# Indices as 16-bit words, and another order of the prologue, in a linear-attention and table-weight layer on eight cores

## What is computed

```python
xn = layernorm(x)
Q = relu(xn @ Wq.T + bq) * decay[n];  K = relu(xn @ Wk.T + bk) * decay[n];  V = xn @ Wv.T + bv
KV = K.T @ V (per head);  Ksum = K.sum(tokens)
att = ((Q @ KV) / (Q @ Ksum + 1e-6)) @ Wo.T + bo
h = silu(xn @ lut[gate_idx].T) * (xn @ lut[up_idx].T)
y = x + att + h @ lut[down_idx].T
```

## Time and profile before

| what | us |
|---|---|
| median of 3 runs (2285.55 to 2312.48) | 2286.12 |
| the profiled execution | 2286.72 |
| its span, slowest core (5) | 2285.1 |
| spans of the eight cores | 2258.1 to 2285.1 |
| TensorE busy | 2113.8 |
| VectorE busy | 1933.5 |
| ScalarE busy | 2006.8 |

### The profile page before, as it was taken

How to read it: one execution, slowest core, us unless ns; L and a number is a source line. 1 busy time by engine, 2 the same in 40 slices (tenths; PEclk the granted TensorE clock), 3 DMA queues, 4 the chain that set the end, 5 groups by cost and what they waited for, 6 DMA issues and landing times.

```text
span 2285.1 us, 32191 instructions; the slowest of 8 cores (2258.1 to 2285.1 us)
## 1 busy us (share of the span) xinstructions
PE 2113.8 (93%) x10561; PEld 985.8 (43%) x10561; DVE 1933.5 (85%) x2274; ACT 2006.8 (88%) x1203; POOL 208.2 (9%) x346
## 2 busy tenths in 40 slices
PE   3999999999989999997899999999999999998965
PEld 1444444444444444443344444444444444443422
DVE  4687888899889898996798999999997898888885
ACT  4799988899889988997699999999999989898895
POOL 2000000000000000001000000000000020202030
PEclk8999999999999999998999999999999999999987
DMA  9961122221222212224724333333336565554522
GB/s 214 199 137 47 57 73 79 79 79 62 77 83 79 88 61 78 79 79 85 137 79 130 119 126 124 122 128 117 130 121 170 149 165 175 145 174 129 152 88 97
DMA packets 71750, 257.74 MB, mean 113 GB/s; under 512 B 9314, under 2 KB 9442, under 8 KB 66338
## 3 DMA queue, kind: packets, MB, share of 16 engines
q0 software_dynamic: 35296, 128.73, 21.2%
q1 hardware_dynamic: 36290, 126.96, 17.3%
HBM read 213.71 MB, written 76.02 MB: 127 GB/s over the span
## 4 chain that ended last, share of the span: by engine, by line
PE 41%; DVEq 23%; DVE 13%; ACT 9%; DMA 6%; issue 6%; SPq 0%; ACTq 0%; POOL 0%; POOLq 0%
PE kvb L964 16%; DVEq L380 13%; PE pp L486 9%; ACT pln L340 8%; PE pp L499 7%; DVE wdec L381 7%; DVEq L508 4%; DVEq L353 3%; PE pp L964 3%; DMA gi<-gidx 3%; DVE st L393 2%; PE pp L945 2%; DVE code L359 2%; DVEq L394 1%; DMA xt<-xb 1%
## 5 line engine op out<-in xcount | busy, mean ns | idle before, releaser
L340 ACT ACTIVATE pln<-gi,bi,sc 128x2048 uint16<-128x2048 int8 x903 | 1832.1, 2086 | 192.2 <-DVE wdec L381 189.8
L381 DVE TENSOR_TENSOR wdec<-wdec,pln 128x2048 uint16<-128x2048 uint16 x903 | 1137.3, 1260 | 128.7 <-ACT pln L340 54.2
L964 PE MATMUL kvb<-xown,wring 128*128 128x512 bf16 x2304 | 508.4, 379 | 0.5 <-DMA wring<-wh 0.5
L486 PE MATMUL pp<-wk_bf,xmid 128*128 128x512 bf16 x1536 | 354.6, 385 | 39.3 <-DVE kbuf L511 38.7
L499 PE MATMUL pp<-wv_bf,xmid 128*128 128x512 bf16 x1536 | 347.2, 379 | 0.7 <-ACT vbuf L518 0.7
L964 PEld LDWEIGHTS kvb<-xown,wring 128*128 128x128 bf16 x2304 | 223.2, 98 | 260.1 <-issue 1.0
L989 PE MATMUL kvb<-w3r,hT 128*128 128x512 bf16 x860 | 216.9, 387 | 51.1 <-DMA w3r<-wh 51.1
L486 PEld LDWEIGHTS pp<-wk_bf,xmid 128*128 128x128 bf16 x1536 | 146.2, 99 | 208.1 <-issue 53.7
L499 PEld LDWEIGHTS pp<-wv_bf,xmid 128*128 128x128 bf16 x1536 | 148.1, 98 | 171.8 <-issue 2.8
L311 POOL DMA_DIRECT2D gi<-gidx x119 | 66.6, 560 | 1522.1 <-ACT pln L340 986.7
L363 DVE TENSOR_SCALAR wdec<-code,hi,lo 128x2048 uint16<-128x2048 uint8 x102 | 138.0, 1353 | 21.5 <-DMA wh<-wdec 6.1
(11 more groups left out here) (112 smaller groups left out, 1446.5 us busy)
## 6 DMA issues: line engine op xcount, KB each, us to landing
wh<-wdec POOLq DMA_DIRECT2D x121, 512.0 KB, 2.9
wring<-wh SPq DMA_DIRECT2D x86, 512.0 KB, 3.4
xt<-xb SPq DMA_DIRECT2D x32, 1024.0 KB, 6.5
gi<-gidx POOLq DMA_DIRECT2D x119, 256.0 KB, 3.0
w3r<-wh SPq DMA_DIRECT2D x43, 512.0 KB, 4.9
wk_bf<-wk POOLq DMA_DIRECT2D x16, 512.0 KB, 31.6
wv_bf<-wv POOLq DMA_DIRECT2D x16, 512.0 KB, 48.6
wq_bf<-wq POOLq DMA_DIRECT2D x16, 512.0 KB, 18.1
```

Source lines behind the costliest of these rows:

```text
L340: scalar.activation(out[:], gi[k % 2][:], AF.Abs, bias=bi8[:, p : p + 1], scale=sc8[:, p : p + 1]).then_inc(s_pl, 1)
L381: vector.tensor_tensor(wdec[k % 2][:], wdec[k % 2][:], pln[(7 * k + m) % NS][:], ALU.min).then_inc(s_mn, 1)
L486: i = tensor.matmul(kb[:], xT(t, dc), wk_bf[:, j, dc, :], start=(dc == 0), stop=(dc == DC - 1))
L964: i = tensor.matmul(bank[g % 6][:], wring[k % 3][:, dc * 128 : (dc + 1) * 128], xown[:, dc, h2 * 512 : (h2 + 1) * 512], start=(dc == 0), s ...
```

## The change

The host doubles each index byte, so that an index is a 16-bit word and a tile's load 512 KB, not 256. The code pass is one AND and OR over 1024 32-bit words: each word becomes a bf16 number whose exponent holds the pair and whose last bit is the bit. The scale of plane i is multiplied by 2^(38-4i), and the bias is the same for all. The pair pass XORs into wdec itself and works there on 16-bit words; the buffer code7 is gone. PL_PRO becomes 8.

In the prologue SyncE loads x0, eye, indices 0, x1 to x3, indices 1, and then dk, bq, epc; tiles 4 to 7 wait only for a free slot. POOL's wv quarter 0 waits for x2, the next quarters for x5. The second half of the transposed tiles 0 to 3 is copied by ScalarE. The transposes of the next tile stand in the middle of a K or V product. VectorE waits for dk before tile 0. Cut to its core (not shown: `v_mm` as `k_mm`; ebase, bi8, sc8 and swi; own_evict_b's choice of engine; the same regrouping on ScalarE and VectorE for tiles 5 to 7, where planes 7 and 8 are made one each):

```diff
-PL_PRO = 10
+PL_PRO = 8
...
-        gi = [sb(es, f"gi{i}", [128, D], I8) for i in range(2)]
+        gi = [sb(es, f"gi{i}", [128, 2 * D], I8) for i in range(2)]
...
-                scalar.activation(out[:], gi[k % 2][:], AF.Abs, bias=bi8[:, p : p + 1],
+                scalar.activation(out[:], gi[k % 2][:].bitcast(BF16), AF.Abs, bias=bi8[:, p : p + 1],
...
-            vector.scalar_tensor_tensor(w32, w32, 4, w32, ALU.logical_shift_left, ALU.bitwise_or)
-            vector.drain()
-            vector.tensor_scalar(w32, w32, -0x1E1E1E1F, None, ALU.bitwise_and).then_inc(s_e, 1)
+            vector.tensor_scalar(w32, w32, 0x0E010E01, 0x30003000, ALU.bitwise_and,
+                                 ALU.bitwise_or).then_inc(s_e, 1)
...
         def dec_pair(vector, k):
-            w32 = gi[k % 2][:].bitcast(I32)
-            vector.drain()
-            vector.tensor_tensor(code7[:], w32, swi[:, 0:1].to_broadcast([128, 512]), ALU.bitwise_xor)
-            vector.drain()
+            w = wdec[k % 2]
             if k >= 2:
                 wh_done(vector, k - 2)
-            vector.tensor_scalar(wdec[k % 2][:], code7[:].bitcast(U8), hi7[:, 0:1], lo7[:, 0:1],
-                                 ALU.mult, ALU.max)
+            vector.drain()
+            vector.tensor_tensor(w[:].bitcast(I32), gi[k % 2][:].bitcast(I32),
+                                 swi[:, 0:1].to_broadcast([128, 1024]), ALU.bitwise_xor)
+            vector.drain()
+            vector.tensor_scalar(w[:], w[:], hi7[:, 0:1], lo7[:, 0:1], ALU.mult, ALU.max)
...
-        def k_mm(tensor, u):
+        def k_mm(tensor, u, nxt=None):
...
+                if nxt is not None and dc == 8:
+                    own_pe(tensor, nxt)
...
             def _(sync):
...
-                for k in range(2):
-                    dec_idx(sync, k)
                 sync.dma_start(out=eye_sb[:], in_=eye_in).then_inc(s_eye, 16)
+                dec_idx(sync, 0)
+                for t in range(1, 4):
+                    sync.dma_start(out=xts[t][:], in_=xb[t * 128 : (t + 1) * 128, :]).then_inc(s_x[t], 16)
+                dec_idx(sync, 1)
                 sync.dma_start(out=dk_sb[:], in_=dkc).then_inc(s_dk, 16)
...
-                for t in range(1, NT):
-                    if t in (2, 3):
-                        sync.wait_ge(s_wk0[2 * t - 4], 16)
-                    elif OT > t >= 4:
+                for t in range(4, NT):
+                    if t < OT:
                         sync.wait_ge(s_xn, 2 * (t - 3))
...
                 gpsimd.dma_start(out=bk_bf[:, 0:512], in_=bk[:, 0:512]).then_inc(s_bk0, 16)
+                gpsimd.wait_ge(s_x[2], 16)
...
                     if j == 1:
-                        gpsimd.wait_ge(s_k, 1)
+                        gpsimd.wait_ge(s_x[1], 32)
...
             def _(scalar):
...
+                for t in range(4):
                     ln_root(scalar, t)
-                    dec_act(scalar, (3, 5, 6, 8)[t - 1])
                     ln_norm_act(scalar, t)
+                    if t > 0:
+                        scalar.wait_ge(s_sc8, 1)
+                        dec_act(scalar, t + 1)
                     own_evict_a(scalar, t)
+                    own_evict_b(scalar, t)
+                ln_root(scalar, 4)
+                ln_norm_act(scalar, 4)
+                dec_act(scalar, 6)
+                v_evict(scalar, 0)
+                own_evict_a(scalar, 4)
...
             def _(vector):
...
                 dec_code(vector, 0)
-                ln_stats(vector, 0)
-                ln_scale(vector, 0)
-                own_evict_b(vector, 0)
                 vector.wait_ge(s_dk, 16)
-                for t in range(1, 5):
+                for t in range(4):
                     ln_stats(vector, t)
                     ln_scale(vector, t)
-                    dec_dve(vector, (3, 5, 6, 8)[t - 1])
+                    if t > 0:
+                        dec_dve(vector, t + 1)
                     if t == 2:
                         vector.wait_ge(s_bk0, 16)
-                    if t in (2, 3):
+                    if t >= 2:
                         k_evict(vector, t - 2)
-                    own_evict_b(vector, t)
...
             def _(tensor):
...
-                for t in range(4):
-                    own_pe(tensor, t)
-                    if t == 0:
-                        tensor.wait_ge(s_sc8, 1)
-                    k_mm(tensor, t)
-                v_mm(tensor, 0)
-                own_pe(tensor, 4)
+                own_pe(tensor, 0)
+                tensor.wait_ge(s_sc8, 1)
+                for t in range(3):
+                    k_mm(tensor, t, t + 1)
+                k_mm(tensor, 3)
+                v_mm(tensor, 0, 4)
...
-        "gidx": gidx, "lut16": f32(L0_ffn_lut).reshape(1, 16),
+        "gidx": np.repeat(gidx, 2, axis=2), "lut16": f32(L0_ffn_lut).reshape(1, 16),
```

More of the change, by code:

```diff
@@ L102, in build @@
     bo = nc.dram_tensor("bo", [128, D], F32, kind="ExternalInput").ap()
[L103 removed]
+    gidx = nc.dram_tensor("gidx", [NK, 128, 2 * D], I8, kind="ExternalInput").ap()
     lut16 = nc.dram_tensor("lut16", [1, 16], F32, kind="ExternalInput").ap()
@@ L421, in own_evict_a, with own_evict_b @@
             scalar.copy(xT_half(t, 0), ps_t[:]).then_inc(s_xa, 1)
-        def own_evict_b(vector, t):
-            vector.wait_ge(s_t, 2 * t + 2)
-            vector.tensor_copy(xT_half(t, 1), ps_u).then_inc(s_xb, 1)
+        def own_evict_b(eng, t):
+            eng.wait_ge(s_t, 2 * t + 2)
+            if t < 4:
+                i = eng.copy(xT_half(t, 1), ps_u)
+            else:
+                i = eng.tensor_copy(xT_half(t, 1), ps_u)
+            i.then_inc(s_xb, 1)
         def own_pe(tensor, t):
@@ L488, in k_mm, with v_mm @@
             i.then_inc(s_k, 1)
-        def v_mm(tensor, u):
+        def v_mm(tensor, u, nxt=None):
             t, j = unit(u)
@@ L674, in _ @@
                 for i in range(8):
-                    gpsimd.memset(ebase[:, i : i + 1], float(32 * i if i < 4 else 32 * i - 256))
+                    gpsimd.memset(ebase[:, i : i + 1], float(2.0 ** (38 - 4 * i)))
                 for i in range(2):
@@ L754, in _ @@
                 v_evict(scalar, 2)
+                dec_act(scalar, 8)
+                ln_root(scalar, 6)
                 own_evict_a(scalar, 5)
-                dec_act(scalar, 10)
-                ln_root(scalar, 6)
                 v_evict(scalar, 3)
@@ L760, in _ @@
                 for u in range(4, NU):
+                    if u in (4, 5):
+                        own_evict_a(scalar, u + 2)
+                    if u == 4:
+                        ln_root(scalar, 7)
+                        ln_norm_act(scalar, 7)
                     if u > 28 and u % 4 == 1 and u < NU - 4:
@@ L799, in _ @@
                 vector.wait_ge(s_cst, 1)
-                vector.tensor_tensor(bi8[:], sc8[:], ebase[:], ALU.mult)
+                vector.scalar_tensor_tensor(bi8[:], sc8[:], -128.0, pr[:, :, 0], ALU.mult, ALU.subtract)
                 vector.drain()
-                vector.scalar_tensor_tensor(bi8[:], bi8[:], -1.0, pr[:, :, 0], ALU.mult, ALU.subtract)
+                vector.tensor_tensor(sc8[:], sc8[:], ebase[:], ALU.mult)
                 vector.tensor_tensor(hi7[:], pr[:, 7:8, 0], pr[:, 7:8, 1], ALU.max)
@@ L840, in _ @@
                         vector.wait_ge(s_bk, 16)
-                    k_evict(vector, u)
                     p, r = OT + (u - 28) // 4, (u - 28) % 4
                     if u == 4:
-                        dec_dve(vector, PL_A[4] - 1)
                         ln_stats(vector, 7)
-                        own_evict_b(vector, 6)
+                    if u in (4, 5):
+                        own_evict_b(vector, u + 2)
+                    if u == 4:
                         ln_scale(vector, 7)
-                    elif u == 5:
-                        dec_dve(vector, PL_A[5] - 1)
-                        own_evict_b(vector, 7)
+                    k_evict(vector, u)
+                    if u in (4, 5):
+                        pass
                     elif u >= 28 and p < NT and r >= 2:
@@ L920, in _ @@
                 kv_mm(tensor, 1)
-                own_pe(tensor, 5)
-                v_mm(tensor, 3)
+                v_mm(tensor, 3, 5)
                 kv_mm(tensor, 2)
                 for u in range(4, NU):
-                    k_mm(tensor, u)
+                    k_mm(tensor, u, u + 2 if u < 6 else None)
                     p, r = OT + (u - 28) // 4, (u - 28) % 4
@@ L930, in _ @@
                     kv_mm(tensor, u - 1)
-                    if u in (4, 5):
-                        own_pe(tensor, u + 2)
                 tensor.wait_ge(s_ke, NU)
```

38 lines of the change are left out of this document (13 added, 25 removed).

## The result

The changed kernel takes 2305.86 us (median of 20 runs) where the kernel before, run beside it, takes 2286.22: a ratio of 1.0061, 95% interval [1.0033, 1.0089]. That is inside the 2% that count as no change, but the interval leaves out 1, so the change costs some 14 us; 2286.1 x 1.0061 is 2300.

What follows compares the result with a forecast made beforehand. VectorE was taken to set the projections by a little, TensorE gate and up, ScalarE's decode the down stage. Terms +20 - 14 + 6 + 2 = +14 us on 2286.7 gave 2301, by the median 2300; range 2270 to 2322.

Steps and rivals of the forecast that it cites:

- Prologue, +20: Prologue: statistics of tile 0 wait for dk, landing at 42 us behind larger loads; +20 us (+4 to +24).
- Codes, -14: Projections: cheaper code passes and an unchanged pair cost relieve VectorE; -14 us over 24 token tiles (4 to 21 saved).
- rival 2: VectorE's pair pass stays at two elements per cycle, so projections win 5 us, not 14: 2311 us; chance 0.18.
- two thirds that were to reach the path: Projections: of 0.86 us less VectorE work per token tile, two thirds, 0.58 us, were to shorten the time.
- Q stage, +6: Start of the Q stage: wq is issued behind a later tile 53, and tile 54 comes later; +6 us (0 to +10).
- Gate and up, 0: Gate and up: TensorE is fully busy, so a faster VectorE buys nothing; 0 us.
- Down, +2: Down stage: two more planes +4, VectorE's relief -3, doubled index load +1; +2 us in all (-4 to +9).
- VectorE's relief there shortens ScalarE's small waits: -3: Down stage: less VectorE work was to shorten ScalarE's small waits, 43.0 us before; -3 us.
- +1 for the doubled load: Down stage: the index load of twice the size beside output traffic was to cost +1 us.
- Rival 1: Prologue: dk lands early and tile 1 lands 10 us sooner, so -10 in place of +20: 2270 us; chance 0.10.
- Rival 3: Every tile: doubled index loads over 5 us hold up the code pass; 46 us on top at 6.6 us, 2346; chance 0.08.
- Rival 4: ScalarE reads bf16 at another price; 0.1 us per plane, 20 us either way in the down stage: 2280 or 2320; chance 0.06.

Runs made afterwards that it cites:

- late wait: The changed kernel with VectorE's wait for dk moved to the first K eviction, where dk is first read: 2275.93 us, ratio 0.9964.
- order-only kernel: The changed kernel with one-byte indices and the old code and pair passes, so only prologue order and PL_PRO 8: 2313.44 us, ratio 1.0129.
- codes alone: The kernel before with 16-bit indices and the new code and pair passes, old prologue and PL_PRO 10: 2272.76 us, ratio 0.9949.
- doubled pass: The changed kernel with every code pass made twice, the second leaving the words as they are: 2339.21 us, ratio 1.0245.
- kernel with the codes and tile 1 first: Old kernel with new codes, eye before the indices, tile 1 before the second index load, dk waited for at first use: 2263.98 us, ratio 0.9911.
- early load: The changed kernel with SyncE issuing dk right behind eye, ahead of the first index load; VectorE's wait unmoved: 2280.38 us, ratio 0.998.
- in pairs: Kernel with the codes and tile 1 first, GpSimd's eight bias additions per quarter spread two behind each of four index tiles: 2258.25 us, ratio 0.9871.

## Why the prediction was right

The forecast was 2300 us, range 2270 to 2322. The median, 2305.86, lies in it, and the ratio gives 2300. The mechanisms of the prologue and of the codes held by themselves; that the sum comes out to the microsecond is partly luck, since several terms were off and cancelled, and one step was wrong.

*Prologue, +20.* Measured +19.0, behind the mechanism named: statistics at 37.91, not 42, ended by the landing of dk. dk took 32.0 us from issue to landing where the sum gave 36. What was too long is the 8.2 us for two small transfers: in the trace the second index load, the last big one ahead of dk, lands at 35.4 (33.9 in the sum) and dk 2.3 us behind it. From dk on, K of tile 0 came 8.75 us later (8.6 forecast) and K of tile 3 38.7 (38). K of tile 4, forecast 26.7 us behind, came 31.3 behind. That term was short by 4.6 and hid that dk's was long by 4: 107.91 against 107, and 139.26 against 137 for tile 8. The late wait shows the same without any stall on dk, 29.3 us against 25.4, so it is the new order itself that is slower there; by what, no run shows. The order-only kernel has the same +18.9, the late wait takes 22.1 back (299.5 to 277.4).

*Codes, -14.* Measured -11.1, and -12.7 with the codes alone. The code pass takes 686 ns (forecast 705), the XOR 1226 (1240), and the TENSOR_SCALAR over the u16 tile:

```profile
L362 DVE TENSOR_SCALAR wdec<-wdec,hi,lo x102: 810/812/1604, 87.9 to 2264.5; 128x2048 uint16<-128x2048 uint16 x102
```

812 ns, where 810 was taken from the argument that the streaming part halves. So the pair costs 2.04 us, as before (the medians were 692 and 1346 ns), and rival 2 (two per cycle) falls. The Trainium skill's rule of four per cycle (VectorE: DVE Perf Modes, What auto-detection actually checks) agrees with the fall from 1346 to 812 ns. The Trainium skill's 693 ns for 2048 elements (VectorE: DVE Perf Modes, Side-by-side: where the cycles go for N=2048 bf16) is 0.12 us less than this form takes, with two operands read from pointers. The two thirds that were to reach the path were nearly right: with the codes alone 12.7 us over 24 tiles are 0.53 of the 0.86 us forecast, and the doubled pass shows 0.81 of 1.22. Why the gain was 11 and not 14 is shown in part: the order costs the projections 3.8 us of its own (order alone), for which the prediction had no term. But -12.7 and +3.8 would leave 8.9, so here too the parts don't simply add. TensorE's wait for the K eviction fell to 20.7 us, not towards 15.

*Q stage, +6.* Measured +3.8 from the last V eviction to the first gate product. TensorE's wait for wq is 23.0 us, about 20 forecast, 13.9 before. Only part of that longer wait is added time.

*Gate and up, 0.* Measured +0.9; TensorE 200.00 of 200 us.

*Down, +2.* Measured +4.0 to the last output addition. The two planes cost 4.2, as forecast, and the last 35 planes still take 69.6 us. The step that failed is "VectorE's relief there shortens ScalarE's small waits: -3". Between Wo and the last plane, ScalarE waited 43.0 us for VectorE in the old kernel and 45.4 in the new one (means over the cores), and 42.9 with the codes alone, whose gain in the stage (3.0 us) is mostly one plane less to make there. Relief in VectorE's passes doesn't reach these waits: in the kernel with the codes and tile 1 first, 14 us of the stage go with GpSimd's additions, and 26 of the 40 us of waits are there without them. So the term of -3 had no ground, and the stage came out dearer than forecast, 4.0 us against 2. The +1 for the doubled load no run prices by itself. One thing stays open here: the order alone, also with eight planes, has a wait of 39.8 and a down stage no longer than before. No run tells why.

*The rivals.* Rival 1, an early dk, did not happen: it landed in the order of issue, behind all that stood ahead of it, and in 6.1 us when it was issued first. The Trainium skill (DMA: Bandwidth & Descriptors, Queues, rings and completion order) warns that completion need not be FIFO; here every transfer of SyncE's queue up to dk landed in the order of issue. The rival's time, 2270, is not far from what the late wait (2275.93) and the early load (2280.38) give, but its price was too good: it counted the 10 us by which tile 1 lands sooner in full, and only 3 of them are left at tile 8. Rival 3: loads of 4.0 us stay under its 5 us, and gate and up don't move. Rival 4: ScalarE's planes are 2086 ns from int8 and from bf16.

## What to carry to other kernels

A wait placed ahead of a loop holds all that the loop does, whatever reads the data: put it at the first reader, and check where the transfer stands in its queue. Here 16 KB behind 5.3 MB cost 22 us and turned a gain of 0.4% into a loss of 0.6%. When two edits come together, run each alone; here one was the gain and the other the loss, and a third kernel with the gain, one load of the other and the late wait beat both. And read the median and the longest of a group beside its mean: a single instruction of 10.49 us in 129 pointed at 14 us in the last stage.

## What was not expected of the hardware

GpSimd and VectorE: beside a row of eight additions of GpSimd (128x512 f32 elements), a VectorE minimum, 1.2 us otherwise, can end only after the row, 10.5 to 11.0 us after its own start. In the kernel with the codes and tile 1 first it happens three times in the down stage on core 0, and so too in the old kernel's profiled core. Two of the three start 0.4 us after the row, but the third is ahead of it by 0.08 us (the row starts at 2035.88, as far as the profile's rough times for GpSimd can tell), so being first doesn't seem to protect it:

```profile
2035.80 11.01 DVE L379 TENSOR_TENSOR wdec<-wdec,pln 128x2048 uint16<-128x2048 uint16 x1 [0.75 <-ACT pln L339]
```

It isn't the minimum alone that is held: on each core of the changed kernel a code pass, 686 ns otherwise, took 9.87 to 10.50 us once. Where VectorE is not held the row is slower instead. In the changed kernel, at the first quarter, eight additions took 16.32 us where a row that holds VectorE takes 9.84:

```profile
1856.84 16.32 POOL L737 TENSOR_TENSOR xo<-xo,bo_q 128x512 f32<-128x512 f32 x8
```

and in that row VectorE's code pass at 1857.53 took 1.77 us and its minima 2.12, while GpSimd's additions rose from 1.3 to up to 2.25. As I read it, the two engines take turns per instruction there, and in the other case GpSimd kept its turn eight times. Of the 32 rows of an execution (four on each core) VectorE is held in 24 in the old kernel and in 9 in the changed one. A row that doesn't hold it costs as well: in the 21 us from a row's start on, ScalarE waits for VectorE 8 us around one that holds and 5.5 around one that doesn't (means of both kernels). The Trainium skill (SBUF — State Buffer, Who interferes with whom) states an exclusive lock for the length of one instruction, the first to issue having it. The rows that alternate fit that; the long minimum fits it only if the lock can pass from one instruction of GpSimd to the next, and the one that starts 0.08 us ahead of the row doesn't fit "the first", if the profile's times are that good. What decides between the two cases no run shows; in pairs no minimum takes over 4.06 us on any core, and they are worth 8.4 us of the down stage.
